# First batch's slot sums as products of rounded parts, in a two-layer transformer kernel on one core

## The reference, cut to what matters

```python
xn = rms_norm(x, gamma_x)                                  # (b, s, d), s = 2048, d = 256
se = rms_norm(slot_embeds, gamma_slot)                     # (e, t, d), e = 8, t = 128
logits = jnp.einsum('bsd,etd->bset', xn, se)
dispatch = jax.nn.softmax(logits, axis=1)                  # over the tokens s
slots = jnp.einsum('bsd,bset->betd', xn, dispatch)         # the slot sums
h = jax.nn.gelu(slots @ w1, approximate=False)
processed = h @ w2
combine = jax.nn.softmax(logits.reshape(b, s, e * t), axis=-1)
out = jnp.einsum('bnd,bsn->bsd', processed.reshape(b, e * t, d), combine)
```

## Time and profile before

| | us |
|---|---|
| median of 3 runs | 1677.43 (1677.25 to 1680.84) |
| profiled execution, its own time | 1678.29 |
| its span | 1676.6 |
| PE busy | 1583.1 (94%) |
| DVE busy | 1188.5 (71%) |
| ACT busy | 776.2 (46%) |

### The profile page before, as it was taken

The page is one execution under the profiler, slowest core; times in us unless marked ns, Lnnn a source line. Parts: engine busy times, 40 slices in busy tenths (PEclk is TensorE's granted clock), DMA queues, the critical chain, the costliest instruction groups (busy, mean ns, idle before and its releaser), DMA issues. The chain is left out here.

```text
span 1676.6 us, 25600 instructions
## 1 busy us (share of the span) xinstructions
PE 1583.1 (94%) x9192; PEld 1368.1 (82%) x9192; DVE 1188.5 (71%) x2656; ACT 776.2 (46%) x1554; POOL 575.2 (34%) x474
## 2 busy tenths in 40 slices
PE   6899989989998999999988999999799999999996
PEld 4689878888888888867867888988688778888895
DVE  6876688764566756746886899989767836666763
ACT  3333333444357134436237878878511314544542
POOL 2100020000000003230436777877400024777764
PEclk9999999999999999999989999999999999999998
DMA  7000000010010000131116232222241125565653
GB/s 232 5 1 1 2 1 1 1 51 1 1 51 26 26 13 13 39 116 70 41 46 210 68 98 79 82 96 79 66 139 52 50 79 165 135 175 136 156 112 38
DMA packets 80885, 115.28 MB, mean 69 GB/s; under 512 B 15692, under 2 KB 60280, under 8 KB 80120
## 3 DMA queue, kind: packets, MB, share of 16 engines
q1 hardware_dynamic: 66808, 95.16, 17.5%
q0 software_dynamic: 12288, 17.31, 5.7%
q10 hardware_dynamic: 1664, 1.18, 0.2%
HBM read 85.32 MB, written 27.68 MB: 67 GB/s over the span
## 5 line engine op out<-in xcount | busy, mean ns | idle before, releaser
L1991 POOL DMA_INDIRECT k_xe<-rows_dram,idx x64 | 82.4, 1287 | 180.0 <-DVE idx L3063 141.7
L3130 POOL DMA_INDIRECT out<-k_eo,idx x64 | 117.0, 1828 | 74.5 <-DVE k_eo L3226 57.3
L1822 PE MATMUL d_pO<-d_sp,d_raw 128*128 128x257 f32 x512 | 116.1, 384 | 1.8 <-DVE x L1256 1.7
L1822 PEld LDWEIGHTS d_pO<-d_sp,d_raw 128*128 128x128 f32 x512 | 96.8, 192 | 16.5 <-DVE x L1256 2.4
L553 ACT ACTIVATE b_p<-b_pS,b_nmax 128x384 f32<-128x384 f32 (+16 forms) x32 | 38.1, 1190 | 132.7 <-DVE b_nmax L694 132.7
L61 PE MATMUL b_pO<-b_vh,b_ph 128*128 128x256 f32 x302 | 87.8, 291 | 6.6 <-DVE b_pl L676 6.4
L62 PE MATMUL b_pO<-b_vh,b_pl 128*128 128x256 f32 x302 | 85.3, 282 | 0.0
L63 PE MATMUL b_pO<-b_vl,b_ph 128*128 128x256 f32 x302 | 85.3, 282 | 0.0
L347 POOL TENSOR_TENSOR x<-x,b_vrow 128x256 f32<-128x256 f32 x32 | 24.2, 787 | 168.7 <-DVE b_hs L622 168.6
L2210 ACT ACTIVATE g_dlm<-d_cumb,mod 128x128 f32<-128x128 f32 x256 | 78.6, 401 | 1.6 <-DMA d_cumb<-cum_dram 1.6
L3185 ACT ACTIVATE k_act_g<-k_pg 128x512 f32<-128x512 f32 x64 | 38.3, 598 | 87.3 <-PE k_pu L63 87.0
(11 more groups left out here) (570 smaller groups left out, 5441.8 us busy)
## 6 DMA issues: line engine op xcount, KB each, us to landing
d_cumb<-cum_dram SPq DMA_DIRECT2D x32, 512.0 KB, 4.2
k_wf<-in_WgT SPq DMA_DIRECT2D x16, 512.0 KB, 3.9
k_wf<-in_WuT SPq DMA_DIRECT2D x16, 512.0 KB, 4.9
k_wf<-in_WdT SPq DMA_DIRECT2D x16, 512.0 KB, 7.0
rows_dram<-h_hx SPq DMA_DIRECT2D x32, 136.0 KB, 3.8
x<-in_x SPq DMA_DIRECT2D x8, 512.0 KB, 9.6
d_w<-in_w SPq DMA_DIRECT2D x4, 1024.0 KB, 6.3
uT_dram<-d_ug SPq DMA_DIRECT2D x16, 256.0 KB, 2.4
```

Source lines behind the costliest of these rows:

```text
L1822: last = nc.tensor.matmul(pO[:, t % 2, 0:PW], raw[e][:, t * P:(t + 1) * P], proc[e], start=e == 0, stop=e == E - 1)
L1991: nc.gpsimd.indirect_dma_start(out=m.xe[:, e % 2, t, :], out_offset=None, in_=m.rows, in_offset=bass.IndirectOffsetOnAxis(ap=column(m, e, ...
L3130: nc.gpsimd.indirect_dma_start(out=out, out_offset=bass.IndirectOffsetOnAxis(ap=column(m, e, t), axis=0), in_=eo[:, e % 2, t, :], in_offse ...
```

## The change

In batch 0 the slot sums become three products of rounded parts (`exact_matmul`), 48 matmuls an expert instead of 16 plain products. Batch 1 stays as it was.

- **Exponentials.** For batch 0 ACT copies all four turned groups, rounded, to `eTh[g % 2]`; DVE subtracts them from the transposed ones in PSUM to get the low part `eTl` (`exps_low`), which it writes over the exponentials in `work`. The semaphore that stood for the copy is now DVE's. The next expert's exponentials on ACT come behind all four copies.
- **Rows.** The normalized rows are split once, in expert 0's round, in six parts (two of 4 tiles, four of 2): ACT rounds them (`rows_high`), DVE subtracts in place (`rows_low`). The high parts need 16 KB of each partition, and take the space of batch 1's residual rows.
- **Parking.** Tiles 24 to 31 are stored during attention, once attention has finished them; tiles 16 to 23 at the start of `soft_mixture`. Tiles 16 to 23 come back behind the spreading of the row maxima, once all slot sums are done; tiles 24 to 31 as before. w2's high part waits for the last slot sum.
- **DVE's order in batch 0.** The maxima of the next expert's groups 0 to 2, then `exps_low` of group 0, then the maximum of group 3 and of the row, then `exps_low` of groups 1 to 3. In the last expert w1's low parts come behind all four `exps_low`.

Cut to its core:

```diff
 # attention, SP
+            sp.wait_ge(s["x_done"], NT - NTB // 2)
+            sp.dma_start(m.x_dram[:, NTB // 2:NTB, :], m.x[:, NT - NTB // 2:NT, :]).then_inc(s["stored"], 16)
 # soft_mixture
-        owner = ["a" if kind == "u" or kind == "exp" and g < 2 else "d" for b, kind, et, g in seq]
+        owner = ["a" if kind == "u" or kind == "exp" and b and g < 2 else "d" for b, kind, et, g in seq]
 # SP
-            sp.dma_start(m.x_dram, m.x[:, NTB:NT, :]).then_inc(s["x_out"], 16)
+            sp.dma_start(m.x_dram[:, 0:NTB // 2, :], m.x[:, NTB:NTB + NTB // 2, :]).then_inc(s["x_out"], 16)
...
             spread_tops(0)
             sp.wait_ge(s["x_out"], 16)
+            sp.wait_ge(s["sl_ready"], E)
+            sp.dma_start(m.x[:, NTB:NT - HT, :], m.x_dram[:, 0:NTB - HT, :]).then_inc(s["x_out"], 16)
+            sp.wait_ge(s["x_out"], 32)
             sp.wait_ge(s["y_ready"], E)
 # DVE
+            def rows_low(i):
+                dve.wait_ge(s["e_high"], high_no["row", i])
+                dve.wait_ge(s["xT_ready"], part_tiles[i][-1] // GT + 1)
+                a, z = high_of(part_tiles[i][0]), high_of(part_tiles[i][-1]) + 1
+                nc.vector.tensor_tensor(low_parts[i], m.xn_parts[i], xn_high[:, a:z].bitcast(F32), ALU.subtract).then_inc(s["xn_done"], 1)
+            def exps_low(et, g):
+                n = at[0, "exp", et, g]
+                dve.wait_ge(s["e_high"], high_no["exp", et * NG + g])
+                nc.vector.tensor_tensor(eTl[:, et % 2, g * GW:(g + 1) * GW], pT[:, n % 2], eTh[g % 2][:].bitcast(F32), ALU.subtract).then_inc(s["t_copied_d"], 1)
...
+                        if et + 1 < E:
+                            for g in range(NG - 1):
+                                bank_maximum(b, et + 1, g)
+                        if et == 0:
+                            rows_low(1)
+                        exps_low(et, 0)
+                        if et + 1 < E:
+                            bank_maximum(b, et + 1, NG - 1)
+                            row_maximum(b, et + 1)
+                        for g in range(1, NG):
+                            exps_low(et, g)
+                            if et == 0 and g + 1 < NG:
+                                rows_low(2 * g)
+                                rows_low(2 * g + 1)
                     if not b and et == E - 1:
+                        for k in range(CH):
+                            first_weights_low(k)
                         slots_low(0)
 # ACT
             def second_weights_high(k):
-                act.wait_ge(s["x_out"], 16)
+                act.wait_ge(s["sl_ready"], E)
...
                 for g in range(NG):
                     keep(b, 0, g)
+                if not b:
+                    rows_high(0)
                 keep(b, 1, 0)
                 exps(b, 0)
+                if not b:
+                    rows_high(1)
...
                     copy_t(b, et, 1)
+                    for g in range(NG if b else 2, NG):
+                        if et == 0:
+                            rows_high(2 * g - 2)
+                            rows_high(2 * g - 1)
+                        copy_t(b, et, g)
                     if et + 1 < E:
                         exps(b, et + 1)
 # PE, slots(b, et, g), for batch 0
+                if not b and et == 0:
+                    pe.wait_ge(s["xn_done"], (1, 2, 4, 6)[g])
+                        last = exact_matmul(nc, pO[:, et % 2, 0:C], eTh[g % 2][:, of], eTl[:, et % 2, t * P:(t + 1) * P],
+                                            xn_high[:, high_of(t)], xn_low[t], begin, end)
```

More of the change, by code:

```diff
@@ L160, in attention @@
         m.xn = [v[:, i, :] for v in (vals0, vals1) for i in range(GT)] + [t for v in (keys0, keys1) for k in range(CH) for t in tiles_of(v, k)]
+        m.xn_parts = [v[:, 0:GT, :] for v in (vals0, vals1)] + [v[:, k, 0:2 * C].rearrange("p (t c) -> p t c", c=C) for v in (keys0, keys1) for k in range(CH)]
         gx, ssx = m.mod[:, 1, GA, :], m.tmp[:, 0:NTB]
@@ L873, in soft_mixture @@
         hid_high = [placed(f"hid_high{j}", [P, 512], area + k * KB, FR) for j, k in enumerate((40, 42, 60, 62, 0, 10, 20, 30))]
+        keys_r = [placed(f"keys{k}r", [P, CH, (NG + 1) * GW], area + 20 * KB * k, FR) for k in range(2)]
+        vals_r = [placed(f"vals{k}r", [P, (NG + 1) * GT, C], area + (40 + 20 * k) * KB, FR) for k in range(2)]
+        low_parts = [v[:, 0:GT, :] for v in vals_r] + [v[:, k, 0:2 * C].rearrange("p (t c) -> p t c", c=C) for v in keys_r for k in range(CH)]
+        part_tiles = [range(0, 4), range(4, 8), range(8, 10), range(10, 12), range(12, 14), range(14, 16)]
+        xn_low = [low_parts[i][:, j, :] for i, some in enumerate(part_tiles) for j in range(len(some))]
+        xn_high = placed("xn_high", [P, NTB, C], m.x_at + NTB * C * 4, FR)
+        high_of = lambda t: (t + NTB // 2) % NTB
+        eTh = [placed(f"eTh{b}", [P, GW], m.x_at + (NT + b * NMOD) * C * 4, FR) for b in range(2)]
         raw += [placed(f"raw{e + 1}", [P, T], area + k * KB) for e, k in enumerate((2, 12, 22, 32, 88, 104, 112))]
         work_at = area + 120 * KB
-        work = placed("work", [P, 2, T], work_at)
+        work, eTl = placed("work", [P, 2, T], work_at), placed("eTl", [P, 2, T], work_at, FR)
         sp_.append(placed("sp1", [P, ES * PW], area + 136 * KB))
@@ L982, in decay_bank @@
             return pL[:, k * GW + j * P:k * GW + j * P + width]
-        owner = ["a" if kind == "u" or kind == "exp" and g < 2 else "d" for b, kind, et, g in seq]
+        owner = ["a" if kind == "u" or kind == "exp" and b and g < 2 else "d" for b, kind, et, g in seq]
+        XN_PARTS = len(part_tiles)
+        highs = [("row", 0), ("row", 1), ("exp", 0), ("exp", 1), ("row", 2), ("row", 3), ("exp", 2), ("row", 4), ("row", 5)]
+        highs += [("exp", i) for i in range(3, E * NG)]
+        high_no = {k: n + 1 for n, k in enumerate(highs)}
         nth = [owner[:n + 1].count(o) for n, o in enumerate(owner)]
@@ L1143, in modulate @@
                     dve.wait_ge(s["stat_powed"], 1)
+                    dve.wait_ge(s["x_out"], 32)
                 if g == NG // 2:
-                    dve.wait_ge(s["x_out"], 32)
+                    dve.wait_ge(s["x_out"], 48)
                 for k in range(GT):
@@ L1191, in turned_low, with bank_maximum, row_maximum @@
                 nc.vector.tensor_tensor(xTl[:, :, cols], staged(b, g), xTh[:, :, cols].bitcast(F32), ALU.subtract).then_inc(s["xT_low"], 1)
+            def bank_maximum(b, et, g):
+                dve.wait_ge(s["raw_done"], bank(b, et, g))
+                nc.vector.reduce_max(part[:, et % 2, g:g + 1], raw[et][:, g * GW:(g + 1) * GW], axis=AX).then_inc(s["part_done"], 1)
             def maxima(b, et):
+                for g in range(NG):
+                    bank_maximum(b, et, g)
+                row_maximum(b, et)
+            def rows_low(i):
[7 more added lines that the diff above has]
+                nc.vector.tensor_tensor(eTl[:, et % 2, g * GW:(g + 1) * GW], pT[:, n % 2], eTh[g % 2][:].bitcast(F32), ALU.subtract).then_inc(s["t_copied_d"], 1)
+            def row_maximum(b, et):
                 n = b * E + et + 1
-                for g in range(NG):
-                    dve.wait_ge(s["raw_done"], bank(b, et, g))
-                    nc.vector.reduce_max(part[:, et % 2, g:g + 1], raw[et][:, g * GW:(g + 1) * GW], axis=AX).then_inc(s["part_done"], 1)
                 dve.wait_ge(s["part_done"], n * NG)
@@ L1410, in _ @@
                 maxima(b, 0)
+                if not b:
+                    rows_low(0)
                 if b:
@@ L1419, in _ @@
                         step_sizes(0, et - 2)
-                    if et + 1 < E:
+                    if b and et + 1 < E:
                         maxima(b, et + 1)
@@ L1423, in _ @@
                         state_offset(0, et - 1)
[L1424 to L1427, removed]
+                    if b:
+                        for g in range(2, NG):
+                            copy_t(b, ("exp", et, g))
+                    else:
+                        if et + 1 < E:
[12 more added lines that the diff above has]
+                                rows_low(2 * g + 1)
                     if not b and et == E - 1:
+                        for k in range(CH):
+                            first_weights_low(k)
                         slots_low(0)
@@ L1579, in copy_t, with rows_high @@
                 act.wait_ge(s["t_ready"], n + 1)
-                nc.scalar.copy(eT[g % 2], pT[:, n % 2]).then_inc(s["t_copied_a"], 1)
+                if b:
+                    nc.scalar.copy(eT[g % 2], pT[:, n % 2]).then_inc(s["t_copied_a"], 1)
+                else:
+                    nc.scalar.copy(eTh[g % 2][:], pT[:, n % 2]).then_inc(s["e_high"], 1)
+            def rows_high(i):
+                if i >= 2:
+                    act.wait_ge(s["x_out"], 16)
+                a, z = high_of(part_tiles[i][0]), high_of(part_tiles[i][-1]) + 1
+                nc.scalar.copy(xn_high[:, a:z], m.xn_parts[i]).then_inc(s["e_high"], 1)
```

(13 more changed lines are left out.)

5 lines of the change are left out of this document (3 added, 2 removed).

## The result

The changed kernel takes 1681.89 us (median of 20 runs) where the kernel before takes 1678.03 in the same session: a ratio of 1.0023, 95% interval [1.0016, 1.003]. The forecast was 1680.9, + 3.5 us; measured are + 3.9, by the interval + 2.7 to + 5.0. It is slower, by little more than can be told from no change.

What follows compares the result with a forecast made beforehand. It took TensorE's own length to bound the kernel in the first batch's dispatch. Terms + 1.5 - 3.9 + 3.1 = + 0.7 us, with 2.8 for the clock + 3.5, on 1677.43 gave 1680.9 us; range 1675.3 to 1685.

Steps and rivals of the forecast that it cites:

- The products: Slot sums on PE: rounded matmuls of 0.118 us, a group 1.50 instead of 1.73, transposes 0.35 instead of 0.43.
- Experts 1 to 6: Middle experts: gain 0.65 us each, 3.9 for six, with PE waiting 0.4 at group 1 and 0.2 at the last.
- Expert 0: First expert, which also splits the row tiles: PE stands still 2.0 us behind DVE's low parts; loss 1.5 us.
- Expert 7 and the way: Last expert to first hidden matmul: low parts queue behind the running maximum and ahead of the last slots' scaling; loss 3.1 us.
- The clock: TensorE's clock falls behind new standstills, two in most executions, expert 0's in half; 0 to 1.7 us each, 2.8 together.
- Parking: Storing tiles and bringing them back on SP's queue: taken as 0, bounded by 3.3 us if transfers share the engines.
- B: Rival on the new standstills: the clock holds or falls once, + 0.7 to + 2.2 us, 1678 to 1679.6; chance 0.22.
- C: Rival on experts 1 to 6: DVE is not in the way, six give 7.0 us, sum - 4.7, 1673; chance 0.14.
- D: Rival on parking: the restoring transfer delays the row maxima by up to 3.3 us, up to 1684.2; chance 0.15.

Runs made afterwards that it cites:

- e3: Changed kernel with DVE doing group 1's low part ahead of the fourth group's maximum and row maximum in experts 1 to 6: 1.0007 against the kernel before, 1678.72 us.
- e8: Changed kernel without the third product (high by low part of the rows), for timing only: 0.9977 against the kernel before, 1674.34 us.
- e5: Changed kernel with the rows split earlier, in eight parts of two tiles, four between expert 0's own logits: 1.0013 against the kernel before, 1679.24 us.
- e2: Changed kernel with matmuls of no use filling PE's three new standstills: 1.0016 against the kernel before, 1679.49 us.
- e4: Changed kernel with expert 7 reordered: low parts before a halved running maximum, w1 rounded between copies, last slots scaled earlier: 0.998 against the kernel before, 1674.17 us.
- e1: Changed kernel run again unaltered: 1.002 against the kernel before, 1681.28 us.
- e9: Changed kernel run unaltered once more, on another comparison's chip: 1.0029 against the kernel before, 1681.41 us.
- e10: The kernel of e2 (matmuls of no use in the three new standstills) run again: 1.0002 against the kernel before, 1677.06 us.
- e6: Kernel before with only the change's transfers (parking and bringing back tiles) and w2's high part waiting for the last slot sum: 1.0001 against the kernel before.
- e7: Changed kernel with the edits of order of e3, e4 and e5 together: 0.9964 against the kernel before, 1670.98 us.
- e11: The kernel of e7 (all three edits of order) run again: 0.9971 against the kernel before, 1672.91 us.
- e12: The kernel of e7 with matmuls of no use in PE's two old standstills, before the third and seventh expert's outputs: 0.9954 against the kernel before, 1669.35 us.

## Why the prediction was right

- **The products.** 0.118 us from start to start and 0.35 for the transposes, as in the earlier trace rows; the plain ones' 0.216 are gone. The Trainium skill's 109 ns ("TensorE: Matmul & The Clock Gate", "Wait — 56ns, not 53.3ns?") did not come out: three matmuls each take from 471.15 to 471.51 and on to 471.86 in after, 0.118 apiece.
- **Experts 1 to 6.** Forecast 0.65 us each, measured 0.63; the two waits at the places named. Their sizes are 0.33 and 0.15 where 0.4 and 0.2 were forecast. e3 shows the first to be DVE's order, e8 that DVE's low parts bound what a shorter PE would bring. Right.
- **Expert 0.** Forecast + 1.5. The first stretch gives + 0.68 with one expert's gain of 0.63 in it, so + 1.3; standstill 1.99 against 2.0. e5 takes it away. Right.
- **Expert 7 and the way.** Forecast + 3.1; + 3.1 with a clock that holds (e2), + 5.7 with the falls. e4 brings it to 0. Right.
- **The clock.** Forecast 2.8, in two places in most executions and in the third in half of them. The two places are in after, e1 and e9. Expert 0's standstill of 2.0 us stands in six profiles (after, e1, e3, e4, e8, e9), and only in e4's was it followed by a fall: fewer than half, as far as six can tell. Within the stage the falls cost 2.6 us in each of the three profiles of the changed kernel; over the whole program e2 and e10 put them between 0.7 and 4.5. Right in kind and within the stage in size. Two things that the forecast left out pull against each other behind the stage: the clock stays low in after up to 499.8, 3.6 us into the hidden matmuls, and an old fall near 512 often does not come.
- **Parking.** Taken as nothing, is nothing (e6).
- **Rivals.** B would have had the clock hold; C wanted over 1.1 us an expert; D a longer wait for the maxima. None came as it was described. (B's upper end, + 2.2 us, lies below the measured interval.)

The size of the change is a small difference of larger terms (- 3.8, + 1.3, + 3.1, and the clock). Without the clock they give + 0.6 where + 0.7 was forecast, and e2 and e10 show that in the profiles: 119.23 and 119.24 against before's 118.57. The rest of + 3.9, some 3.2 us, is the clock's, of which 2.6 are seen in the stage and the remainder is not traced. That the sum came within 0.4 us is partly luck: the result's own interval is wider than that, and the clock's term over the whole program is known to some 2 us only.

## What to carry to other kernels

Splitting an operand on two more engines makes a chain of three engines out of a copy of one, and what it costs is decided by what stands ahead in those engines' queues: go through each queue at the first and the last turn of the loop, where the pattern breaks, not only in the middle. Here each middle turn gained 0.63 us and the two ends lost 4.4, and a change of order alone turned the kernel from + 0.2% to - 0.3%. A standstill of TensorE of some 2 us in otherwise dense work can cost more than its length (here the two standstills around expert 7 cost another 2.6 us by two falls of the clock); ask if other work can be put into it.

## What was not expected of the hardware

TensorE's clock fell behind standstills as short as 1.98 us (e4, expert 0: granted clock 0.54 and 0.61 over 388 to 392) and stayed up behind one of 1.99 at the same place in after and e1. In e7 it fell behind two short ones of 0.96 and 0.52 us with transposes of 0.44 between (0.72 and 0.50 over 486 to 490), in e11, the same kernel, it stayed up behind the same two. The same kernel therefore has falls at other places in other executions, which may be much of the 3 to 10 us by which the executions of one kernel differ: among those of one kernel, 0.001 less of the mean granted clock goes with some 1.0 us more time (an estimate, fitted over the 236 executions on record). By the same numbers the changed kernel's mean clock is 0.9842, that of e2 and e10 0.9862, that of the kernel before 0.9864. The Trainium skill ("TensorE: Matmul & The Clock Gate", "What's actually happening") says that the throttle is the default and activity releases it; e2, e10 and e12, where matmuls of no use kept the clock at full in the stretches that they were put into, agree. On the way to the feed-forward the clock stayed low for 6.8 us in after, twice as long as in expert 7, with PE busy 1.48 of 2 us and then all the time; the forecast had reckoned with one fall there as short as that of the earlier trace rows.
